# Six in-place states and GpSimd step inputs for seven recurrence units of a two-layer kernel on one Trainium2 core

## What is computed

```python
h = x @ fc1_w.T + fc1_b
xc, z = split(h @ in_proj_w.T)
u = silu(causal_conv4(xc) + conv_b)
dt_low, Bm, Cm = split(u @ x_proj_w.T)              # 8, 16, 16 columns
dt = softplus(dt_low @ dt_proj_w.T + dt_proj_b)     # (batch, 1024, 256)
h_t = exp(dt_t * A) * h_{t-1} + (dt_t * u_t) * B_t  # state (256, 16)
y_t = sum_n h_t[:, n] * C_t[n]
y = (y + u * D) * silu(z)
out = (y @ out_proj_w.T) @ fc2_w.T + fc2_b
```

## Time and profile before

| what | us |
|---|---|
| median of three runs | 1117.55 |
| lowest and highest | 1115.35, 1117.87 |
| the profiled execution's own time | 1121.12 |
| its span, first to last instruction | 1119.8 |
| PE busy in the span | 1066.3 |
| DVE busy | 839.1 |
| POOL busy | 763.4 |
| ACT busy | 630.4 |

### The profile page before, as it was taken

How to read it: one execution, slowest core, us unless ns; L and a number is a source line. 1 busy time by engine, 2 the same in 40 slices (tenths; PEclk the granted TensorE clock), 3 DMA queues, 4 the chain that set the end, 5 groups by cost and what they waited for, 6 DMA issues and landing times.

```text
span 1119.8 us, 18526 instructions
## 1 busy us (share of the span) xinstructions
PE 1066.3 (95%) x6860; PEld 662.1 (59%) x6860; DVE 839.1 (75%) x1234; ACT 630.4 (56%) x898; POOL 763.4 (68%) x394
## 2 busy tenths in 40 slices
PE   7999999999999999999999999779789987999998
PEld 4555665665665655665665657767344433446786
DVE  6876976776765775766975748235999999997987
ACT  5554655654644654643554635348986646757663
POOL 5788788787787897877899830230789897994200
PEclk9999999999999999999999999889899999999999
DMA  7000000000000000000000253465565443440000
GB/s 213 1 2 2 1 2 1 2 2 1 2 2 2 1 1 2 2 2 1 6 7 6 77 178 94 136 215 151 182 206 165 143 161 132 147 154 20 10 10 19
DMA packets 55369, 68.91 MB, mean 62 GB/s; under 512 B 23248, under 2 KB 41424, under 8 KB 55280
## 3 DMA queue, kind: packets, MB, share of 16 engines
q1 hardware_dynamic: 52272, 64.65, 18.7%
q0 software_dynamic: 1024, 2.10, 0.6%
q10 hardware_dynamic: 1984, 0.98, 0.3%
HBM read 61.30 MB, written 6.16 MB: 60 GB/s over the span
## 4 chain that ended last, share of the span: by engine, by line
PE 79%; issue 7%; DVE 6%; POOL 4%; ACT 3%; DMA 1%; another core or an unknown queue 1%; POOLq 0%; DVEq 0%; ACTq 0%
PE psum L661 20%; PE psum L622 16%; PE psum L647 6%; PE psum L635 5%; PE psum L1046 3%; PE psum L687 3%; PE psum L952 3%; PE psum L1029 3%; POOL hc L2252 3%; PE psum L746 3%; PE psum L702 2%; PE psum L810 2%; PE psum L821 2%; PE psum L726 2%; PE psum L680 2%
## 5 line engine op out<-in xcount | busy, mean ns | idle before, releaser
L2164 POOL TENSOR_TENSOR psums<-psums,prob 128x1024 f32<-128x1024 f32 x180 | 430.5, 2392 | 26.1 <-POOL psums L2164 0.5
L1627 DVE TENSOR_REDUCE mx<-psum 128x2 f32<-128x1024 f32 x256 | 299.8, 1218 | 102.0 <-PE psum L647 101.6
L1158 ACT ACTIVATE prob<-psum 128x1024 f32<-128x1024 f32 x256 | 261.3, 1026 | 62.6 <-PE psum L635 38.1
L661 PE MATMUL psum<-prob,V 128*64 128x512 f32 x1024 | 238.7, 597 | 0.0
L2252 POOL TENSOR_TENSOR hc<-hs,cc 128x1024 f32<-128x1024 f32 x64 | 151.6, 2368 | 21.1 <-DVE hs L1930 18.6
L1930 DVE TENSOR_TENSOR_SCAN hs<-dA,psum 128x1024 f32<-128x1024 f32 x64 | 146.3, 2287 | 2.2
L661 PEld LDWEIGHTS psum<-prob,V 128*64 128x64 f32 x1024 | 67.7, 137 | 106.7 <-issue 105.0
L2164 POOL TENSOR_TENSOR psums<-prob 128x1024 f32<-128x1024 f32 x30 | 72.1, 2403 | 85.0 <-ACT prob L1158 84.2
L1177 ACT COPY oraw<-psum 128x512 f32<-128x512 f32 x32 | 18.8, 587 | 191.3 <-PE psum L661 191.3
L952 PE MATMUL psum<-hc,ident 128*128 128x512 f32 x256 | 122.5, 601 | 2.8 <-DVE slot_rows_h L1938 1.4
L647 PE MATMUL psum<-k_hi,q_hi 64*128 64x512 f32 x512 | 107.0, 409 | 1.7 <-DVE mx L1627 1.3
(11 more groups left out here) (319 smaller groups left out, 1712.6 us busy)
## 6 DMA issues: line engine op xcount, KB each, us to landing
cc<-C_rows SPq DMA_DIRECT2D x64, 512.0 KB, 3.8
kq_wts<-in_e_rows SPq DMA_DIRECT2D x14, 578.0 KB, 4.2
e_wts<-in_e_rows SPq DMA_DIRECT2D x10, 578.0 KB, 3.9
e_w<-in_e_rows SPq DMA_DIRECT2D x6, 578.0 KB, 5.1
slots_in<-e_zero SPq DMA_DIRECT2D x2, 960.0 KB, 7.1
inv<-sum_rows SPq DMA_DIRECT2D x120, 1.0 KB, 2.0
slots_out<-e_y SPq DMA_DIRECT2D x30, 64.0 KB, 1.8
e_w<-in_e_w SPq DMA_DIRECT2D x1, 1024.0 KB, 7.0
```

The costliest lines, as they stand in the source:

```text
L661: ins = pe.matmul(A.O[HALF[s], :], A.V[pair % 2][:, j, s * DH:(s + 1) * DH], A.prob[unit(pair, c, j) % NPB][:, s * CH:(s + 1) * CH], start ...
L1158: act.activation(A.prob[n % NPB][:, :], slots.bank("score", pair, c, j).rearrange("p s n -> p (s n)"), ACT.Exp, scale=float(DH) ** -0.5).t ...
L1627: dve.tensor_reduce(K.A.mx[:, :, t, c], slots.bank("max", pair, t, c), AXX, ALU.max).then_inc(*slots.inc("max", pair, t, c))
L2164: pool.tensor_tensor(total[:, :], (K.A.prob[(n - 1) % NPB] if j == 1 else total)[:, :], K.A.prob[n % NPB][:, :], ALU.add).then_inc(*K.psum ...
```

## The change

- **Ring of states.** `hc` is gone. `hs` has six tiles (`NHS = 6`), POOL multiplies the state in place, and the scan of unit u waits for PE's add of unit u-6 (before: for POOL's product of u-3). POOL no longer waits for PE's adds. PE adds three units behind (`ADD_LAG = 3`), and `leave(0, 0)` and `leave(0, 1)` with their `gated` come one unit later.
- **Seven gains on POOL.** For units 19, 23, 41, 44, 48, 56, 61 PE spreads no B and DVE does no multiplication. SP copies row B_n from DRAM over all partitions (one DMA of 512 KB) into one of two tiles, POOL multiplies it by du right behind its product of unit u-4, and the decay of these units is written to the PSUM banks that the gain would have used, so that the scan reads dA from PSUM and the gain from SBUF. ACT may write it only when the scan of u-2 is done. The copy is issued by SP in unit max(15, u-6, ...), behind the C copy of that unit.
- **C_rows** also holds the B rows: 128 KB instead of 64 KB per batch.
- **Norm 6** is done by halves like norm 5: sums on ACT, roots on POOL in three short steps per half, nothing on DVE. Its transposes stay at units 43 (PE) and 44 (ACT).
- **Step sizes sooner.** `dtp`, `softexp`, `softlog`, `dt`, `du` of (1, 1) move from units 40 to 45 to units 30 to 38.
- **fc2bias** (POOL): batch 0 moves from unit 21 to before the recurrence, batch 1 from unit 43 to unit 21.
- **Low parts** of the first weights: units 47, 49, ..., 59 instead of 47 to 54; of the second weights only four in units 60 to 63, four in the dense stage.
- The start-up memsets count on one semaphore instead of four.

```diff
+NHS, ADD_LAG = 6, 3
+POOL_GAINS = (19, 23, 41, 44, 48, 56, 61)
+GAIN_AHEAD = 4
+B_FROM = 15
+def copied_at(i):
+    return max(B_FROM, POOL_GAINS[i] - 6, POOL_GAINS[i - 2] + 1 if i >= 2 else 0)
 def pe_spread_B(K, pe, u):
+    if u in POOL_GAINS:
+        return
 def pe_unit(K, pe, u):
-    if u > 1:
-        pe_add_state(K, pe, u - 2)
+    if u >= ADD_LAG:
+        pe_add_state(K, pe, u - ADD_LAG)
 def act_decay(K, act, u):
-    if u >= 3:
+    if u in POOL_GAINS:
+        act.wait_ge(X.state_done, u - 1)
+    elif u >= 3:
         act.wait_ge(X.state_done, u - 2)
-    act.activation(X.dA[u % 3][:, :], X.dt[b][:, k, :], ACT.Exp, ...)
+    act.activation(decay_of(X, u), X.dt[b][:, k, :], ACT.Exp, ...)
 def dve_unit(K, dve, u):
+    if u in POOL_GAINS:
+        gain = X.B_copy[POOL_GAINS.index(u) % 2]
+    else:
+        dve.tensor_tensor(gain, gain, (X.du if u else X.dt)[b][:, k, :], ALU.mult)
+    if u in POOL_GAINS:
+        dve.wait_ge(X.pool_gained, gains_by_pool(u))
-    if u >= 3:
-        dve.wait_ge(X.product_done, u - 2)
+    if u >= NHS:
+        dve.wait_ge(X.added, u - NHS + 1)
+    dve.tensor_tensor_scan(X.hs[u % NHS][:, :], decay_of(X, u), gain, 0.0, ALU.mult, ALU.add)
+def pool_gain(K, pool, u):
+    pool.wait_ge(X.du_done, KI * b + k + 1)
+    pool.wait_ge(X.B_copied[i % 2], 16 * (i // 2 + 1))
+    pool.tensor_tensor(X.B_copy[i % 2], X.B_copy[i % 2], X.du[b][:, k, :], ALU.mult)
 def pool_unit(K, pool, u):
-    if u >= 3:
-        pool.wait_ge(X.added, u - 2)
-    pool.tensor_tensor(X.hc[u % 3][:, :], X.hs[u % 3][:, :], X.cc[u % NCC][:, :], ALU.mult)
+    pool.tensor_tensor(X.hs[u % NHS][:, :], X.hs[u % NHS][:, :], X.cc[u % NCC][:, :], ALU.mult)
+    if u + GAIN_AHEAD in POOL_GAINS:
+        pool_gain(K, pool, u + GAIN_AHEAD)
+def sp_copy_B(K, sp, i):
+    sp.wait_ge(X.C_stored, 16 * (b + 1))
+    ...
+    sp.dma_start(X.B_copy[i % 2], X.C_rows[b, n, :].partition_broadcast(P))
 recurrence_order, one = {
-  17: [("leave", 0, 0), ("gated", 0, 0), ("mix", 1, 2, 0), ("mix", 1, 3, 0)],
+  17: [("mix", 1, 2, 0), ("mix", 1, 3, 0)],
-  18: [("silu", 1, 0, 0), ("silu", 1, 1, 0)],
+  18: [("leave", 0, 0), ("gated", 0, 0), ("silu", 1, 0, 0), ("silu", 1, 1, 0)],
-  33: [("leave", 0, 1), ("gated", 0, 1)], 35: [("outp", 0, 0)],
+  30: [("dtp", 1, 1)], 31: [("dtp_out", 1, 1)], 32: [("softexp", 1, 1), ("softlog", 1, 1)],
+  34: [("leave", 0, 1), ("gated", 0, 1)], 35: [("outp", 0, 0)], 36: [..., ("dt", 1, 1)],
-  38: [("fc2", 0, 1), ("fc2_out", 0, 0)], 39: [("fc2_out", 0, 1)],
-  40: [("lnvar", 6), ("lnroot", 6), ("dtp", 1, 1)], 41: [("dtp_out", 1, 1), ("lnrows", 6)],
-  43: turned(6)[:2] + [("softexp", 1, 1), ("softlog", 1, 1), ("fc2bias", 1)],
+  38: [..., ("du", 1, 1)], 39: [("fc2_out", 0, 1), ("means", 2), ("centre", 2)],
+  40: [("squares", 2), ("halfroot", 2), ("means", 3), ("centre", 3)], 41: [("halfrows", 2)],
+  42: [("squares", 3), ("halfroot", 3)], 43: [("halfrows", 3)] + turned(6)[:2],
+  W1_LOW = {e: 45 + 2 * e for e in range(1, E1)}
```

More of the change, by code:

```diff
@@ L82, with gains_by_dve, gains_by_pool @@
 SKIP_AT = {1: 14, 2: 11, 3: 11}
+POOL_GAINS = (19, 23, 41, 44, 48, 56, 61)
+GAIN_AHEAD = 4
+B_FROM = 15
+def gains_by_dve(u):
+    return sum(v not in POOL_GAINS for v in range(u + 1))
+def gains_by_pool(u):
+    return sum(v in POOL_GAINS for v in range(u + 1))
+def copied_at(i):
+    return max(B_FROM, POOL_GAINS[i] - 6, POOL_GAINS[i - 2] + 1 if i >= 2 else 0)
 class Signal:
@@ L357, in first_inputs_order @@
     s = NSLOT
-    order = turned(4) + [("down", s + 4), ("fc1", 0), ("fc1_out", 0), ("yrow", s + 4), ("fetch", s + 10)]
+    order = turned(4) + [("down", s + 4), ("fc1", 0), ("fc1_out", 0), ("fc2bias", 0), ("yrow", s + 4), ("fetch", s + 10)]
     order += [("down", s + 5), ("up", s + 6), ("gelu", s + 6), ("inp", 0, 0), ("inp_out", 0, 0), ("yrow", s + 5), ("fetch", s + 11)]
@@ L383, in recurrence_order @@
            13: [("mix", 0, 3, 0)], 14: [("lnturn", 5, 1), ("lncopy", 5, 1)], 15: [("fc1", 1, 1), ("fc1_out", 1, 1)],
[L384 to L386 removed]
+           16: [("mix", 1, 0, 0), ("mix", 1, 1, 0)], 17: [("mix", 1, 2, 0), ("mix", 1, 3, 0)],
@@ L387, in recurrence_order @@
+           18: [("leave", 0, 0), ("gated", 0, 0), ("silu", 1, 0, 0), ("silu", 1, 1, 0)], 19: [("mix", 0, 0, 1), ("mix", 0, 1, 1)], 20: [("mix", 0, 2, 1)],
+           21: [("mix", 0, 3, 1), ("mix", 1, 0, 1), ("fc2bias", 1)], 22: [("mix", 1, 1, 1)], 23: [("mix", 1, 2, 1), ("mix", 1, 3, 1)],
            24: [("silu", 1, 0, 1), ("silu", 1, 1, 1), ("xpj", 1, 0)], XDR_UNIT: [("xpj", 1, 1), ("xpj_out", 1), ("xdr", 1)],
-           26: [("dtp", 1, 0), ("dtp_out", 1, 0)], 27: [("softexp", 1, 0)], 28: [("softlog", 1, 0), ("dt", 1, 0)], 29: [("du", 1, 0)],
@@ L389, in recurrence_order @@
[L389 to L392, removed]
+           26: [("dtp", 1, 0), ("dtp_out", 1, 0)], 27: [("softexp", 1, 0)], 28: [("softlog", 1, 0), ("dt", 1, 0)], 29: [("du", 1, 0)], 30: [("dtp", 1, 1)], 31: [("dtp_out", 1, 1)], 32: [("softexp", 1, 1), ("softlog", 1, 1)],
@@ new lines, in recurrence_order @@
+           34: [("leave", 0, 1), ("gated", 0, 1)], 35: [("outp", 0, 0)], 36: [("outp_out", 0, 0), ("outp", 0, 1), ("dt", 1, 1)], 37: [("outp_out", 0, 1), ("fc2", 0, 0)],
+           38: [("fc2", 0, 1), ("fc2_out", 0, 0), ("du", 1, 1)], 39: [("fc2_out", 0, 1), ("means", 2), ("centre", 2)], 40: [("squares", 2), ("halfroot", 2), ("means", 3), ("centre", 3)],
+           41: [("halfrows", 2)], 42: [("squares", 3), ("halfroot", 3)], 43: [("halfrows", 3)] + turned(6)[:2],
+           44: turned(6)[2:] + [("inp", 1, 2)], 45: [("inp_out", 1, 2)], 46: [("inp", 1, 3)],
@@ L393, in recurrence_order @@
            47: [("inp_out", 1, 3), ("w1hi", 0), ("w1lo", 0), ("xhi", 0, 0), ("xlo", 0, 0)], 55: [("xhi", 0, 1), ("xlo", 0, 1)]}
     for e in range(E1):
-        one[48 + e - 1] = one.get(48 + e - 1, []) + [("w1hi", e), ("w1lo", e)] * (e > 0)
-        one[56 + e] = [("w2hi", e), ("w2lo", e)]
+        one[48 + e - 1] = one.get(48 + e - 1, []) + [("w1hi", e)] * (e > 0)
+        one[56 + e] = [("w2hi", e)] + [("w2lo", e - 4)] * (e >= 4)
+    for e in range(1, E1):
+        one[W1_LOW[e]] += [("w1lo", e)]
@@ L971, in pe_unit @@
         pe_spread_B(K, pe, u + 1)
-    if u > 1:
-        pe_add_state(K, pe, u - 2)
+    if u >= ADD_LAG:
+        pe_add_state(K, pe, u - ADD_LAG)
     if u == RECS:
-        pe_add_state(K, pe, u - 1)
+        for v in range(RECS - ADD_LAG + 1, RECS):
+            pe_add_state(K, pe, v)
 def pe_outp(K, pe, b, c):
@@ L2414, in sp_unit @@
         sp_spread_C(K, sp, u + NCC - 1)
+    for i in range(len(POOL_GAINS)):
+        if u == copied_at(i):
+            sp_copy_B(K, sp, i)
 def sp_added(K, sp, b, c):
```

137 lines of the change are left out of this document (83 added, 54 removed).

## The result

The changed kernel takes 1125.05 us (median of 1121.50, 1124.05, 1126.04 and 1127.65), the kernel before 1116.82 beside it: a ratio of 1.0062, 95% interval 1.0045 to 1.0078. It is slower, by some 7 us, and 2 us above the top of the predicted range (1123.0).

The account below looks back on a forecast made before the run. POOL was taken as the bound after the change: 4.7 us saved without pauses against pauses of 6.45 us, so product 63 ends 1.8 us later. That gave 1119.4 us against the median of 1117.55, range 1114.3 to 1123.0.

Parts of the forecast that it names:

- What costs nothing: Ring of six, ACT sums of norm 6, seven copies, PSUM decays, later leave, C_rows store, semaphores, earlier step sizes: no charge.
- the walk: POOL's queue from 849.50 to product 63: pauses of 6.45 us against 4.7 us saved, so product 63 ends 1.8 us later.
- pause for copy 19: POOL before gain 19: the copy lands after 5.1 us, so POOL stands 3.0 us; 1.2 at a landing of 3.3.
- POOL becomes the bound: Recurrence: POOL gets net +12.1 us of 16.8 fillable, so DVE's 10.9 us cannot all appear and each POOL pause costs.
- step 4: Norm 6: second halfroot ends at 952.5 behind POOL's backlog, gain 45 starts at 955.6; waits 0.8 and 0.95 at scans 46, 47.
- Add 16 waits for the later leave, but product 16 is later still: PE's add 16: waiting for the later leave costs nothing, as product 16 comes later.
- Steps 4 to 6: From norm 6 on: POOL waits 0.8 and 0.95 at scans 46, 47, 0.55 at expert 1's low part, 0.35 at 52 and 55.
- POOL without most pauses: Rival: copy 19 lands after 3.3 us and norm 6's chain comes in time; 1114.0 to 1115.6 us, chance 0.22.
- The first rival: POOL bound with pauses as walked: 1119.4 us, from 1117.5 to 1121.8; chance 0.5.
- DVE stays the bound: Rival: POOL keeps up in the recurrence and DVE's 10.9 us appear, 1106.7 us, or part of them; chance 0.08.
- The slower rival: Copy 19 lands late, between product 15 and gain 19 on POOL; 1122.5 us at the worst landing of 8.2; chance 0.2.
- The lock: Port lock between GpSimd and DVE reading two SBUF tiles: nothing charged, as these seven units' decay is in PSUM.

Follow-up runs that it names:

- e10: Changed kernel plus dummy matmuls on PE, shorter than its waits, ahead of three waits at norm 5 and norm 6; ratio 1.0029 to the kernel before.
- e15: Changed kernel with six gains on POOL, unit 19 multiplied by DVE again; ratio 1.0030 to the kernel before.
- e2: Changed kernel, seven gains kept, norm 6 again with statistics on DVE and one root on POOL; ratio 1.0017 to the kernel before.
- e5: Changed kernel with no gains on POOL and norm 6 statistics on DVE, adds still three behind; ratio 1.0034 to the kernel before.
- e7: As e5, with adds two units behind and leave and gated where they were; ratio 0.9995 to the kernel before.
- e13: e5 plus 8 dummy matmuls on PE ahead of the transposes of norm 5; ratio 1.0008 to the kernel before.
- e3: Changed kernel with adds two units behind again, leave and gated one unit earlier; ratio 1.0047 to the kernel before.
- e1: Changed kernel with all seven gains back on DVE, the rest kept; ratio 1.0035 to the kernel before.
- e4: Changed kernel with only the gains of units 56 and 61 on POOL; ratio 1.0008 to the kernel before.

## Why the prediction was wrong

The direction of the sum was right (later, not sooner) and the engine too; the size was not: +1.8 us forecast, +7.6 in the profiles. The failed step is "What costs nothing": PE's granted clock and the adds three behind have no term in the sum, so they stood at nothing, and the clock at norm 5 and norm 6 alone measured 3.7 us (e10). With the pauses of PE at norm 5 and norm 6 filled, the changed kernel stands at 1.0029, some 3.2 us above the kernel before, within the predicted range and near the +1.8 of the walk; in part by luck, as its profiled execution is still 4.5 us longer in the recurrence than the kernel before. Step by step, times behind the first scan (790.49 before, 783.30 after); the forecasts are the prediction's times less 790.49.

| step | forecast | measured |
|---|---|---|
| pause for copy 19 | 3.0 | 2.82 |
| start of gain 19 | 64.4 | 65.3 |
| xdr | 98.2 | 99.5 |
| gain 32 | 115.1 | 116.5 |
| product 34's wait | 0.45 | 0.75 |
| end of the second halfroot | 162.0 | 165.1 |
| gain 45 | 165.1 | 168.9 |
| waits at 46, 47 | 0.8, 0.95 | 2.42, 1.08 |
| low part of expert 1 | 0.55 | 1.36, and 0.43 for expert 0 |
| waits at 52 and 55 | 0.35 each | none |
| end of product 63 | 232.7 | 238.5 |

**"POOL becomes the bound": right, and shown.** Taking gain 19 off it gives 3.6 us (e15), the halves of norm 6 off it 5.0 (e2). The chain that step 4 walked, roots behind POOL's backlog, ACT's scaling, PE's transposes, the spread of B 45, is in the trace as written. Copy 19 took what the row of a copy behind a copy said.

**"What costs nothing" failed.** It held the later `leave`, and nothing at all about the adds three units behind or PE's clock. By e5 and e7 the adds and the leave cost 4.4 us without gains, 2.9 of them through the clock at norm 5 (e13), and 1.7 with the gains (e3, within the intervals). By e10 the half clock at norm 5 and norm 6 costs 3.7 us in the changed kernel. It shows in the first rows of the table: scan 12 was 1.5 us late before any part of my walk began, and with the filler 1.1 of it were gone. These sizes overlap and do not add up.

**"Add 16 waits for the later leave, but product 16 is later still": not quite.** PE stood 0.64 us for the `leave` and began add 16 at 853.72, 0.4 us behind the end of product 16 (850.92 + 2.36):

```profile
853.72 1.98 PE L980 MATMUL psum<-hs,ident 128*128 128x512 f32 x4 [0.64 <-ACT du L1451]
```

`gated` waits for the leave too and stands in POOL's queue: at 913.81 it held POOL 1.10 us, in front of the roots of norm 6. But the later `leave` alone does not do that. POOL stood there in two profiles, this one and e2 (0.90), and in both the matmuls ahead of that leave ran at the half clock throughout (3.62 us for the four of L977, above). In e1, e4, e5 and e15, with the same later `leave`, those four took 1.88 us and POOL did not wait. In e15:

```profile
903.97 1.88 PE L977 MATMUL psum<-u,skip 128*128 128x512 f32 x4
...
912.65 2.34 POOL L2280 TENSOR_TENSOR du<-du,zg 128x1024 f32<-128x1024 f32 x1
```

In e10, where they took 2.95, it did not wait either. So this term goes with the clock as well.

**Step 4's sum was short by 3.8 us**: 1.4 were inherited from gain 32, 1.7 came between it and the halfroot (0.3 at product 34, 1.1 at `gated`), 0.7 behind the halfroot, where ACT and a PE at half clock took 3.7 instead of 3.1.

**Steps 4 to 6 behind gain 45 were short by another 2.0**: between the spreads of B 45 and B 46 PE had one unit's adds, still partly at the half clock (2.80 us instead of 1.88), and an input projection, so gain 46 came 1.23 late, and product 63 took 0.44 longer beside the splits.

**The rivals.** "POOL without most pauses" needed the norm's chain in time; it came 3.8 us later still. The first rival's upper end, 1121.8, was 0.6 above what its own margin gives (1119.4 + 90 x 0.02 = 1121.2); it makes no difference to the outcome. "DVE stays the bound" fell with POOL's first windows. The slower rival named the landing of copy 19 as its mechanism; it landed in 4.72 us, and the slowdown came from elsewhere. I had no rival for PE, though the change lengthens its pauses; that is the case that was missing.

**The lock.** No scan of a POOL-gain unit slowed a product: 2.26 to 2.29 us with one operand in PSUM, products beside them 2.35 to 2.38. At the very end product 63 took 2.80 while DVE split (2.33 instead of 0.69 for the longest split); before, a split took 2.13 beside product 63, which had started first and kept its 2.36.

## What to carry to other kernels

Work moved to an engine with an eighth of its time free (20.5 of 171 us) is free only where the receiving engine stands waiting at that very place: two gains at units 50 and 56 bring 3 us, seven spread over units 19 to 61 lose 5. Before putting a reordering at nothing, list the idle stretches of TensorE that it lengthens, and read the granted clock behind each; a few dummy matmuls ahead of such a wait, shorter than the wait, test it in one run. And look at every queue in which the consumers of a step stand: matmuls at the half clock made a `leave` late, and through `gated` this held POOL, ahead of a norm that another engine needed.
